# Expert scatter before gather, list products in slot zero, and the order of the last output parts

## The chip, the cores and the metric

The kernel runs on one core of one Trainium2 chip. The metric is the device time of one execution in microseconds (us), smaller being better: 1261.15 us is the median of three executions of the kernel before (1260.3 to 1261.98). The chip's engines are named PE (TensorE, matrix products), DVE (VectorE), ACT (ScalarE), POOL (GpSimd) and SP (SyncE, which here only issues DMAs). Each runs its own instructions strictly in order and waits for others by semaphores.

## The reference, cut to what matters

The input `x` is 4 x 2048 x 256. It is normalised, and two branches read the result; the output is their sum with `x`.

```
xn = layernorm(x)
# attention branch: H = 8 heads, DK = 128, DV = 64, gated linear attention
q, k, v = xn@Wq, xn@Wk / sqrt(DK), xn@Wv ;  alpha = sigmoid((xn@Wg + bg) / 16)
state = alpha*state + k v^T ;  out_t = q . state           # a scan over 2048 tokens
attn  = (out * sigmoid(xn@Wog)) @ Wo
# expert branch: E = 64 experts, 8 chosen per token, at most CAP = 256 tokens per expert
topk  = grouped top-8 of sigmoid(xn @ gate_w.T) + gate_bias
buf[e]= the first 256 tokens that chose e, in token order
y[e]  = (silu(buf[e]@w_gate[e]) * (buf[e]@w_up[e])) @ w_down[e]
ffn[token] += y[e, slot] * weight[token, e]
out   = x + attn + ffn
```

## The kernel before, in words

The 2048 tokens of each batch are cut into C = 16 chunks of 128, and one *step* c = 0..15 handles one chunk of all four batches for the attention. A step has a slot zero (the first projections, and the output projection `out_proj` of the chunk before) and slots s = 1..8, one per head. Other work stands *beside* the attention in fixed places of the slots: every engine has its own function `beside(c, kind, s, place)`, called at numbered places, and this hand-written table alone sets the order.

- Steps 0 to 4, kind "norm": the layer norm and the routing of three chunks each.
- Step 5, "count": counts of the chosen tokens.
- Step 6, "slots": the lists of token numbers, 16 *list products* of four experts each. PE's `slots_of_four` (L777) does the products, DVE's `count_four` (L1479, L1480, L1482, and L1470 for half of the comparisons of a later product) reads them, and POOL's `reach_group` (L659) does the other half of the comparisons. `FOUR_AT` is the table of their (slot, place). They use two banks in turn, and two buffers. At the end of the step `make_lists` (L1492 to L1499) writes the lists, and POOL may gather.
- Steps 7 to 14, "experts": eight experts each, one per slot. For expert e, PE transposes its gathered tokens (`expert_tokens`, L927, at slot e%8 + 1, place 0), makes the hidden layer (L937), and the down product (L948) one slot later. DVE's `expert_out` (L1622) weights the result into the buffer `yb`.
- Step 15, "last": the last chunk. Behind it `out_part` (L914) projects the outputs of chunk 15, in parts by head pairs, batch by batch, and DVE (L1585) adds the rest and SP writes each batch out.

POOL moves the tokens of the experts. `gather(e)` (L627) is two indirect DMAs that read 128 rows of 1280 bytes each from `table`; `scatter(e)` (L635) is two indirect DMAs that add 128 rows of 1024 bytes each to `acc`. PE's `expert_tokens` of e waits for both halves of `gather(e)`. The token buffer `xg` has two halves, so `gather(e + 2)` waits until ACT has read the last of expert e (`share_kept`, L1160). `deliver(e)` waits for DVE's `y_cp`, then until the scatter of the expert before has landed (the rows of two experts may be the same), and then issues `scatter(e)`. For the first expert of a step it first issues `add_attention` (L653), a DMA that adds a chunk's attention output, 512 KB, to `acc`, and waits for its landing (`att_added`). SP loads the experts' weights and the decay tables (`decay`, L405, and `carry`, L411, 512 KB each) on another queue.

Of the kernel before, what the change touches and what calls it, by code (L numbers as in the profile page):

```python
# [23 lines left out]
KO = HV // P  # L24
# [31 lines left out]

COUNT_AT = [(s, 2) for s in range(2, H + 1)] + [(H, 3)]
assert len(COUNT_AT) == E // CB
FOUR_AT = [(s, place) for s in range(1, H) for place in ((0, 4, 2) if s == 4 else (0, 2))] + [(H, 0)]
FOUR_AT.sort(key=lambda at: (at[0], (0, 1, 2, 4, 3).index(at[1])))  # L60
assert len(FOUR_AT) == E // EB
NORM_CHAIN = 3
ROUTE_LINKS = (7, 4, 3, 5)
# [14 lines left out]
def build(nc, x_in, Wq, Wk, Wv, Wo, Wg, bg, Wog, gate_w, gate_bias, w_gate, w_up, w_down, out):  # L78
    with ExitStack() as ctx:
# [281 lines left out]
        def is_last(c):  # L361
            return isinstance(c, int) and c == C - 1
# [191 lines left out]
        def _(pool):  # L554
# [126 lines left out]
                scatter(e)  # L681

            for e in range(E):
                pool.wait_ge(share_kept, e + 1)
                gather(e + 2)
                if e > 0:
                    deliver(e - 1)
            deliver(E - 1)

# [2 lines left out]
        def _(pe):  # L692
# [199 lines left out]
            def out_proj(c, b):  # L892

                to = out_bank(c, b)
                if b == 0:
                    pe.wait_ge(g_low, 4 * c)
                if isinstance(c, int) and c == C - 1:
                    pe.wait_ge((ut_cp, state_up)[b // 2], 4 * (C - 1))
                elif b == 1:
                    pe.wait_ge(state_up, 4 * c)  # L900
                elif b > 1:
                    pe.wait_ge(wo_cp, 4 * (c - 1) + b - 1)
                for j in range(KO):
                    for i, (part, other) in enumerate(PARTS):
                        last = mm(to, gT[:, part, j, b * P:(b + 1) * P], wo[:, other, j, :],  # L905
                                  start=(j + i == 0), stop=(j == KO - 1 and i == 2))
                last.then_inc(wo_ps, 1)
# [70 lines left out]
            def step(c, kind):  # L978
# [13 lines left out]
                proj_qk(c, kind, 0, 1)  # L992
                if not first:
                    out_proj(c, 0)
                proj_v(c, kind, 2)
                if not first:
                    out_proj(c, 1)
                if not is_last(c):
                    keys_back(c, 0)
                scores(c, 0)  # L1000
                if kind in ("experts", "last") and not (isinstance(c, int) and c == E0):
                    expert_down(c - 1, STEP_E - 1)
                proj_v(c, kind, 3)
                if not first:
                    out_proj(c, 2)
                for s in range(1, H + 1):
                    if s > 1 and not is_last(c):
                        keys_back(c, s - 1)
# [41 lines left out]
            step(C - 1, "last")  # L1050
            out_part(2, (0, 1, 2))
            out_part(3, (0, 1, 2))
            out_part(0, (2,))
            out_part(1, (2,))
            for b in range(B):
                out_part(b, (KO - 1,))


        @block.scalar
# [227 lines left out]
        def _(dve):  # L1287
# [338 lines left out]
            def beside(c, kind, s, place):  # L1626
# [29 lines left out]
                if kind == "count" and s > 0:  # L1656
# [2 lines left out]
                            keep_group(COUNT_AT.index((s, pe_place)))  # L1659
                    if place == 3 and s == H:  # L1660
                        keep_totals()
                if kind == "slots" and s == 0 and place == 3:
                    keep_firsts()
                if kind == "slots" and (s, place) in FOUR_AT:
                    count_four(FOUR_AT.index((s, place)))
# [21 lines left out]
            def step(c, kind):  # L1687
                beside(c, kind, 0, 0)
                beside(c, kind, 0, 1)
                if kind != "experts":  # L1690
                    beside(c, kind, 0, 3)
                if kind in ("experts", "last") and not (isinstance(c, int) and c == E0):
                    hidden_low(c - 1, STEP_E - 1)
                    down_low(c - 1, STEP_E - 1)
                if not is_first(c) and not is_last(c):
                    projected(c, 0, kind)
                    projected(c, 1, kind)
                beside(c, kind, 0, 4)
                for s in range(1, H + 1):
                    if kind == "experts":  # L1700
                        keys_weighted(c, s - 1)
# [2 lines left out]
                        expert_out(c - 1, STEP_E - 1)  # L1704
                    if s == 1 and kind == "experts":
                        weights_low_e(c, 0)
                    if s == 1 and not is_first(c) and not is_last(c):
                        projected(c, 2, kind)
                        if kind == "experts":
                            tokens_low_e(c, 0)  # L1710
                        projected(c, 3, kind)
# [76 lines left out]
```

## Time and profile before

| | |
|---|---|
| three executions, median | 1261.15 us |
| the profiled execution's own time | 1266.82 us |
| its span in the trace | 1265.1 us |
| PE busy | 1237.9 us, 98% |
| DVE busy | 976.6 us, 77% |
| ACT busy | 624.3 us, 49% |
| POOL busy | 487.4 us, 39% |
| chain that ended last | PE 76%, DVE 16%, issue 5% |

Times in the rows are microseconds from the span's start. The step "slots" runs from 453.5 to 524.2 us, the first step with experts begins there, and the second runs from 608.2 to 692.1 us. The profiled execution is 5.67 us above the median of the three others. The releaser that a row names behind an idle time is the one that came last by the profile.

### The profile page before, as it was taken

To read this page: it belongs to the slowest core of one execution; us is meant where nothing else is said; L and a number is where in the kernel's file an instruction comes from. 1 tells how busy PE (TensorE), PEld (TensorE's weight loads), DVE (VectorE), ACT (ScalarE), POOL (GpSimd) and SP (SyncE) were. 2 spreads that over 40 slices of the span, in tenths; PEclk is the share of its full clock that TensorE was granted. 3 is DMA by queue.
4 is the path that set the end of the run, shared out by engine and by line. 5 is a ranking of instruction groups with operands and counts; after the bars stand their busy time and mean duration, and the time that the engine had idled before them with its cause. 6 is when DMAs were issued, how large, how long until landed. Compare 5 with 4: busy or idle time off the path is not lost.

```text
span 1265.1 us, 28662 instructions
## 1 busy us (share of the span) xinstructions
PE 1237.9 (98%) x9910; PEld 1092.2 (86%) x9910; DVE 976.6 (77%) x2343; ACT 624.3 (49%) x1319; POOL 487.4 (39%) x377
## 2 busy tenths in 40 slices
PE   7899999999999999999999999999999999999999
PEld 6788888887888888799899998989989999889987
DVE  6997878889797659878688687786885877868844
ACT  6675756666574544344444444444444444434432
POOL 2110111011001027237467385474574754845620
PEclk9999999999999999999999999999999999999999
DMA  6576534354352322357486575674774765748665
GB/s 241 170 250 200 188 110 156 122 190 158 121 171 60 111 75 84 95 145 186 105 198 165 130 178 136 150 181 106 188 171 121 172 155 137 193 104 191 162 194 183
DMA packets 124920, 194.68 MB, mean 154 GB/s; under 512 B 12016, under 2 KB 98608, under 8 KB 124592
## 3 DMA queue, kind: packets, MB, share of 16 engines
q1 hardware_dynamic: 94384, 147.99, 36.1%
q0 software_dynamic: 30464, 45.83, 19.7%
q8 instruction: 34, 0.56, 0.2%
q14 instruction: 38, 0.31, 0.1%
HBM read 148.62 MB, written 57.74 MB: 163 GB/s over the span
## 4 chain that ended last, share of the span: by engine, by line
PE 76%; DVE 16%; issue 5%; ACT 2%; another core or an unknown queue 0%; DVEq 0%; DMA 0%; ACTq 0%
PE bank L793 21%; PE bank L808 7%; PE bank L905 7%; PE bank L937 7%; PE bank L845 6%; PE bank L825 5%; PE bank L877 3%; PE bank L863 3%; PE bank L866 3%; PE bank L948 3%; PE bank L836 3%; DVE Dt L1506 3%; PE bank L889 2%; PE bank L927 2%; DVE At L1527 2%
## 5 line engine op out<-in xcount | busy, mean ns | idle before, releaser
L635 POOL DMA_INDIRECT acc<-arena,idx_all x128 | 224.3, 1752 | 149.4 <-DMA acc<-res 54.1
L627 POOL DMA_INDIRECT arena<-table,idx_all x132 | 163.6, 1240 | 153.8 <-ACT share L1160 96.5
L793 PE MATMUL bank<-xp,wq 128*128 128x512 f32 x768 | 208.4, 406 | 0.0
L793 PE MATMUL bank<-xp,wk 128*128 128x512 f32 x768 | 202.2, 398 | 0.0
L793 PEld LDWEIGHTS bank<-xp,wk 128*128 128x128 f32 x768 | 138.5, 188 | 29.3 <-DVE wk L1416 0.4
L793 PEld LDWEIGHTS bank<-xp,wq 128*128 128x128 f32 x768 | 136.6, 189 | 25.4 <-issue 0.8
L1506 DVE TENSOR_TENSOR_SCAN Dt<-decay,eye_b 128x512 f32<-128x512 f32 x128 | 157.7, 1233 | 0.0
L845 PE MATMUL bank<-qT,kT 128*128 128x128 f32 x1024 | 136.2, 275 | 1.8 <-DVE At L1527 1.4
L1136 ACT ACTIVATE kT<-bank 128x512 f32<-128x512 f32 x128 | 76.7, 599 | 118.0 <-PE bank L793 102.2
L845 PEld LDWEIGHTS bank<-qT,kT 128*128 128x128 f32 x1024 | 125.2, 192 | 3.3 <-DVE At L1527 1.6
L1136 ACT ACTIVATE qT<-bank 128x512 f32<-128x512 f32 x128 | 76.9, 601 | 85.4 <-PE bank L793 64.7
L1527 DVE TENSOR_TENSOR At<-bank,Dt 128x512 f32<-128x512 f32 x128 | 87.7, 685 | 27.9 <-PE bank L845 26.3
L601 POOL DMA_DIRECT2D table<-arena x16 | 12.4, 777 | 248.4 <-DVE arena L1400 232.8
L937 PEld LDWEIGHTS bank<-xgT,wgu_p 128*128 128x128 f32 x768 | 98.6, 188 | 10.4 <-issue 5.7
L863 PE MATMUL bank<-At,V 128*64 128x128 f32 x1024 | 98.7, 273 | 6.4 <-DVE At L1527 6.4
L937 PE MATMUL bank<-xgT,wgu_p 128*128 128x256 f32 x768 | 102.4, 282 | 2.2 <-issue 2.0
L808 PE MATMUL bank<-wv,xp 128*128 128x512 f32 x384 | 103.2, 404 | 0.8 <-DVE xp L1410 0.7
L825 PE MATMUL bank<-xp,wog 128*128 128x512 f32 x384 | 101.8, 400 | 0.0
L905 PEld LDWEIGHTS bank<-wo,gT 128*128 128x128 f32 x720 | 93.3, 188 | 5.5
L905 PE MATMUL bank<-wo,gT 128*128 128x256 f32 x720 | 94.6, 280 | 0.0
L866 PE MATMUL bank<-carry,state 128*64 128x128 f32 x960 | 94.1, 273 | 0.0
L1154 ACT ACTIVATE gT<-gated 128x512 fp32r<-128x512 f32 x64 | 40.4, 630 | 91.5 <-DVE gated L1549 79.1
(174 smaller groups left out, 2317.1 us busy)
## 6 DMA issues: line engine op xcount, KB each, us to landing
decay<-decay_dram SPq DMA_DIRECT2D x64, 512.0 KB
carry<-decay_dram SPq DMA_DIRECT2D x60, 512.0 KB
arena<-in_L_attn_x_dram SPq DMA_DIRECT2D x16, 512.0 KB, 4.5
table<-arena SPq DMA_DIRECT2D x16, 512.0 KB, 3.2
xT_dram<-arena SPq DMA_DIRECT2D x16, 512.0 KB, 3.0
arena<-in_L_ffn_w_gate_dram SPq DMA_DIRECT2D x64, 128.0 KB
arena<-in_L_ffn_w_up_dram SPq DMA_DIRECT2D x64, 128.0 KB
arena<-in_L_ffn_w_down_dram SPq DMA_DIRECT2D x64, 128.0 KB
```

The lines of the kernel that those rows point to most:

```text
L627: pool.indirect_dma_start(out=xg[:, e % 2, j, :], out_offset=None, in_=table[:, :], in_offset=bass.IndirectOffsetOnAxis(ap=idx_all[:, e, j ...
L635: pool.indirect_dma_start(out=acc[:, :], out_offset=bass.IndirectOffsetOnAxis(ap=idx_all[:, e, j:j + 1], axis=0), in_=yb[:, e % 2, j, :], ...
L793: last = mm(to[:, :], w[:, part, k, h * DK:(h + 1) * DK], xp[:, other, k, :], start=(k + i == 0), stop=(k == KD - 1 and i == 2))
L808: last = mm(to[:, :], xp[:, part, k, b * P:(b + 1) * P], wv[:, other, k, :], start=(k + i == 0), stop=(k == KD - 1 and i == 2))
L825: last = mm(to[:, :], wog[:, part, k, j * P:(j + 1) * P], xp[:, other, k, :], start=(k + i == 0), stop=(k == KD - 1 and i == 2))
L845: last = mm(bank[2][:, b * P:(b + 1) * P], kT[:, h % 2, b * P:(b + 1) * P], qT[:, h % 2, b * P:(b + 1) * P], start=True, stop=True)
L863: last = mm(bank[5][u * DV:(u + 1) * DV, b * P:(b + 1) * P], V[:, b, h * DV:(h + 1) * DV], At[:, u, b, :], start=True, stop=is_first(c))
L866: last = mm(bank[5][u * DV:(u + 1) * DV, b * P:(b + 1) * P], state[:, 2 * p + u, b, :], carry[:, p % 2, u, b, :], start=False, stop=True)
L905: last = mm(to, gT[:, part, j, b * P:(b + 1) * P], wo[:, other, j, :], start=(j + i == 0), stop=(j == KO - 1 and i == 2))
L937: last = mm(expert_bank[j % 2][:, m * CAP:(m + 1) * CAP], wgu_p[:, part, m, k * I:(k + 1) * I], xgT[:, other, k * CAP:(k + 1) * CAP], star ...
L1136: f(dst[:, h % 2, :], bank_of(kind, "qk"[which], h)[:, :], ACT.Copy, scale=scale).then_inc(qk_cp, 1)
L1506: dve.tensor_tensor_scan(Dt[:, h, :, :].rearrange("p b t -> p (b t)"), decay[:, (h // 2) % 2, (h % 2) * BP:(h % 2 + 1) * BP], eye_b[:, :, ...
```

## The change

It has three parts, and none changes what is computed.

1. POOL, in the experts' loop: for every expert e except those with e % 8 == 1, `deliver(e - 1)` is called before the wait for `share_kept` and `gather(e + 2)`; before, it was called behind them. With e % 8 == 1 (where `deliver(e - 1)` has the attention's DMA in it) the order stays.
2. The step "slots": four of the 16 list products move into slot zero, at new places 2 to 5 on PE and DVE; the last of them is now at slot 7, place 0. DVE's `keep_firsts` is called at place 1 instead of 3; its place in DVE's order is the same.
3. After the last step PE does parts 2 and 3 of batch 0 together, then of batch 1, then part 3 of batches 2 and 3. Before, part 2 of batches 0 and 1 came first, and then part 3 of all four.

```diff
-FOUR_AT = [(s, place) for s in range(1, H) for place in ((0, 4, 2) if s == 4 else (0, 2))] + [(H, 0)]
+FOUR_AT = [(0, place) for place in range(2, 6)] + [(1, 2)]
+FOUR_AT += [(s, place) for s in range(2, H - 1) for place in (0, 2)] + [(H - 1, 0)]
...
             for e in range(E):
+                slow = e % STEP_E == 1
+                if e > 0 and not slow:
+                    deliver(e - 1)
                 pool.wait_ge(share_kept, e + 1)
                 gather(e + 2)
-                if e > 0:
+                if slow:
                     deliver(e - 1)
...
                 if not first:
                     out_proj(c, 0)
+                beside(c, kind, 0, 2)
                 proj_v(c, kind, 2)
                 if not first:
                     out_proj(c, 1)
+                beside(c, kind, 0, 3)
...
                     projected(c, 0, kind)
+                    beside(c, kind, 0, 2)
                     projected(c, 1, kind)
-                beside(c, kind, 0, 4)
+                beside(c, kind, 0, 3 if kind == "slots" else 4)
...
-            out_part(0, (2,))
-            out_part(1, (2,))
             for b in range(B):
-                out_part(b, (KO - 1,))
+                out_part(b, (2, KO - 1) if b < 2 else (KO - 1,))
```

POOL's order from the first expert on, before. L627 is a gather half, L635 a scatter half, L653 the attention's DMA; in brackets is what the instruction waits for.

```order
L627 DMA arena<-table,idx_all 128x320 [waits share_kept]
L627 DMA arena<-table,idx_all 128x320
L653 DMA acc<-res 128x4x256 [waits init_acc,wo_cp]
L635 DMA acc<-arena,idx_all 8448x256 [waits att_added,y_cp]
L635 DMA acc<-arena,idx_all 8448x256
L627 DMA arena<-table,idx_all 128x320 [waits share_kept]
L627 DMA arena<-table,idx_all 128x320
L635 DMA acc<-arena,idx_all 8448x256 [waits y_cp,scattered]
L635 DMA acc<-arena,idx_all 8448x256
L627 DMA arena<-table,idx_all 128x320 [waits share_kept]
```

These are the gather of expert 3, the attention, the scatter of 0, the gather of 4, the scatter of 1, and the gather of 5 begins. The same place of the kernel after:

```order
L627 DMA arena<-table,idx_all 128x320 [waits share_kept]
L627 DMA arena<-table,idx_all 128x320
L653 DMA acc<-res 128x4x256 [waits init_acc,wo_cp]
L635 DMA acc<-arena,idx_all 8448x256 [waits att_added,y_cp]
L635 DMA acc<-arena,idx_all 8448x256
L635 DMA acc<-arena,idx_all 8448x256 [waits y_cp,scattered]
L635 DMA acc<-arena,idx_all 8448x256
L627 DMA arena<-table,idx_all 128x320 [waits share_kept]
L627 DMA arena<-table,idx_all 128x320
L635 DMA acc<-arena,idx_all 8448x256 [waits y_cp,scattered]
```

The scatter of expert 1 now stands directly behind that of expert 0, and the gather of expert 4 behind both.

PE's order in slot zero of the step "slots" and the slot behind it, before. L905 is `out_proj`, L777 a list product (bank 7 and bank 4 in turn), L808 and L793 projections, L836 and L845 the keys and scores.

```order
L905 MATMUL bank5<-wo,gT 128x256 x12
L808 MATMUL bank0<-wv,xp 128x512 x6
L905 MATMUL bank6<-wo,gT 128x256 x12
L836 MATMUL bank3<-ident,kT 128x128 x4
L845 MATMUL bank2<-qT,kT 128x128 x4
L808 MATMUL bank1<-wv,xp 128x512 x6
L905 MATMUL bank5<-wo,gT 128x256 x12
L777 MATMUL bank7<-arena,sel_all 128x64 x8
L793 MATMUL bank0<-xp,wq 128x512 x6
L905 MATMUL bank6<-wo,gT 128x256 x12
L793 MATMUL bank1<-xp,wk 128x512 x6
L777 MATMUL bank4<-arena,sel_all 128x64 x8
```

And after; each line's number is 3 higher there.

```order
L908 MATMUL bank5<-wo,gT 128x256 x12
L780 MATMUL bank7<-arena,sel_all 128x64 x8
L811 MATMUL bank0<-wv,xp 128x512 x6
L908 MATMUL bank6<-wo,gT 128x256 x12
L780 MATMUL bank4<-arena,sel_all 128x64 x8
L839 MATMUL bank3<-ident,kT 128x128 x4
L848 MATMUL bank2<-qT,kT 128x128 x4
L780 MATMUL bank7<-arena,sel_all 128x64 x8
L811 MATMUL bank1<-wv,xp 128x512 x6
L908 MATMUL bank5<-wo,gT 128x256 x12
L780 MATMUL bank4<-arena,sel_all 128x64 x8
L796 MATMUL bank0<-xp,wq 128x512 x6
```

Four products now stand ahead of the projections of slot 1 (the last row), where before there was one.

## Rows read from the trace of the kernel before

**Rows 1.** The page: busy time of each engine.

```profile
PE 1237.9 (98%) x9910; PEld 1092.2 (86%) x9910; DVE 976.6 (77%) x2343; ACT 624.3 (49%) x1319; POOL 487.4 (39%) x377
```

**Rows 2.** Waits, whole span: waiter, releaser, us in total, times, longest.

```profile
POOL acc L635 <- DMA acc<-res: 54.1, 8, 7.9
```

**Rows 3.** Stretches of two expert steps: PE, PEld, DVE, ACT, POOL busy, clock, DMA.

```profile
608.20:692.10 83.90, 83.90 (x676) 76.06 (x674) 64.73 (x117) 37.81 (x82) 50.23 (x33) 1.00 0.66 157
692.10:777.30 85.20, 84.49 (x674) 75.96 (x672) 64.75 (x117) 37.47 (x82) 51.56 (x34) 1.00 0.65 153
```

**Rows 4.** Timeline of PE, end of step "slots": start, duration, [idle before, releaser].

```profile
521.89 0.44 PE L863 MATMUL bank<-At,V 128*64 128x128 f32 x4 [1.77 <-DVE At L1527]
```

**Rows 5.** Timeline of DVE, same place.

```profile
512.32 0.48 DVE L1470 TENSOR_SCALAR sel_all<-arena 128x256 bf16<-128x256 bf16 x2
...
518.73 0.66 DVE L1479 TENSOR_TENSOR arena<-bank,slot_col 128x504 bf16<-128x504 f32 x1
...
519.42 0.68 DVE L1482 TENSOR_REDUCE arena<-arena 128x8 f32<-128x504 bf16 x1
...
521.15 0.69 DVE L1527 TENSOR_TENSOR At<-bank,Dt 128x512 f32<-128x512 f32 x1
```

**Rows 6.** Timeline, all engines, slot zero of step "slots".

```profile
457.75 3.75 POOL L659 TENSOR_SCALAR sel_all<-arena 128x256 bf16<-128x256 bf16 x4 [46.97 <-DVEq L1463]
...
459.39 1.58 PE L905 MATMUL bank<-wo,gT 128*128 128x256 f32 x12
...
471.08 0.42 DVE L1589 TENSOR_TENSOR res<-bank,addend 128x256 f32<-128x256 f32 x1 [2.71 <-PE bank L905]
```

**Rows 7.** Timeline of POOL, expert step c = 9, experts 0 to 5 of it.

```profile
729.27 2.48 POOL L635 DMA_INDIRECT acc<-arena,idx_all  x1 [6.75 <-DMA acc<-res]
732.06 1.58 POOL L635 DMA_INDIRECT acc<-arena,idx_all  x1 [0.31 <-issue]
...
735.86 1.07 POOL L627 DMA_INDIRECT arena<-table,idx_all  x1 [0.30 <-issue]
737.23 2.37 POOL L635 DMA_INDIRECT acc<-arena,idx_all  x1 [0.30 <-issue]
739.90 1.57 POOL L635 DMA_INDIRECT acc<-arena,idx_all  x1 [0.30 <-issue]
...
743.55 1.54 POOL L627 DMA_INDIRECT arena<-table,idx_all  x1 [0.30 <-issue]
```

**Rows 8.** Timeline, same step: PE's tokens of expert 4, DVE's result of expert 2.

```profile
738.07 0.85 DVE L1622 TENSOR_SCALAR arena<-bank,share 128x256 f32<-128x256 f32 x2
...
743.84 0.60 PE L927 MATMUL bank<-ident,arena 128*128 128x128 f32 x4
```

**Rows 9.** DMA queues, 735.65 to 736.25 (only one has packets): packets, MB, share.

```profile
q1 hardware_dynamic: 198, 0.10, 56.7%
```

**Rows 10.** DMA, 713.2 to 714.0, and POOL's last issue before it.

```profile
DMA packets 0, 0.00 MB, mean 0 GB/s; under 512 B 0, under 2 KB 0, under 8 KB 0
...
710.44 1.07 POOL L627 DMA_INDIRECT arena<-table,idx_all  x1 [0.31 <-issue]
```

**Rows 11.** DMA queues, 743.9 to 748.4, then 748.4 to 750.0.

```profile
q0 software_dynamic: 142, 0.37, 36.4%
...
DMA packets 99, 0.08 MB, mean 53 GB/s; under 512 B 17, under 2 KB 99, under 8 KB 99
```

**Rows 12.** Timeline, step c = 10: POOL's scatter of expert 0, PE's tokens of expert 4.

```profile
816.62 1.55 POOL L635 DMA_INDIRECT acc<-arena,idx_all  x1 [0.31 <-issue]
...
829.14 0.60 PE L927 MATMUL bank<-ident,arena 128*128 128x128 f32 x4
```

**Rows 13.** Timeline, end of the program.

```profile
1257.56 4.49 PE L914 MATMUL bank<-wo,gT 128*128 128x256 f32 x36
...
1259.07 0.69 DVE L1570 TENSOR_TENSOR gT<-gated,gT 128x512 fp32r<-128x512 f32 x1 [0.70 <-ACT gT L1154]
...
1261.49 1.81 SPq L547 DMA_DIRECT2D out_dram<-qT  x4
```

More of the change, by code:

```diff
@@ L58 @@
 assert len(COUNT_AT) == E // CB
-FOUR_AT = [(s, place) for s in range(1, H) for place in ((0, 4, 2) if s == 4 else (0, 2))] + [(H, 0)]
-FOUR_AT.sort(key=lambda at: (at[0], (0, 1, 2, 4, 3).index(at[1])))
+FOUR_AT = [(0, place) for place in range(2, 6)] + [(1, 2)]
+FOUR_AT += [(s, place) for s in range(2, H - 1) for place in (0, 2)] + [(H - 1, 0)]
 assert len(FOUR_AT) == E // EB
@@ L1002, in step @@
                     expert_down(c - 1, STEP_E - 1)
+                beside(c, kind, 0, 4)
                 proj_v(c, kind, 3)
@@ L1005, in step @@
                     out_proj(c, 2)
+                beside(c, kind, 0, 5)
                 for s in range(1, H + 1):
@@ L1661, in beside @@
                         keep_totals()
-                if kind == "slots" and s == 0 and place == 3:
+                if kind == "slots" and s == 0 and place == 1:
                     keep_firsts()
@@ L1689, in step @@
                 beside(c, kind, 0, 1)
-                if kind != "experts":
+                if kind in ("norm", "count"):
                     beside(c, kind, 0, 3)
@@ L1706, in step @@
                         weights_low_e(c, 0)
+                    if s == 1 and kind == "slots":
+                        beside(c, kind, 0, 4)
                     if s == 1 and not is_first(c) and not is_last(c):
                         projected(c, 2, kind)
+                        if kind == "slots":
+                            beside(c, kind, 0, 5)
                         if kind == "experts":
```

## The prediction

> **What bounds the kernel now.** I read the engines' busy times first, then the stretches of single steps, the list of waits, and last the timelines of the three places that the change touches. PE is busy 98% of the span [rows 1]. In an expert step such as c = 8 PE has no idle time at all: 83.90 of 83.90 us [rows 3]. So PE is the bound nearly everywhere. A change pays only where it closes one of the few gaps in PE's order, and whatever makes PE wait in an expert step is added to the end in full. POOL is busy 50 us of such a step [rows 3], and waits some 7 us in each for the attention's DMA (54.1 us in eight) [rows 2]; it has slack on the average, and the question is whether it has it where the gathers are due.
>
> **Part 2, list products in slot zero.** At the end of the step "slots" PE stands 1.77 us until 521.89, waiting for DVE's masked scores At [rows 4]. DVE is why: it comes to At only at 521.15, behind a list product that held it from 518.73 to 519.42 + 0.68 = 520.10 [rows 5]. A list product costs DVE these 1.37 us and 0.48 for two comparisons (L1470) of a later one [rows 5], about 1.9 us in all. Four of them leave slots 1 to 8, so DVE has some 7.6 us less in a stretch at whose end it is about 2 us late. The stall goes; next in line is then PE's own order. What takes the four in? In slot zero DVE waits for each of the four `out_proj`, 2.71 us for the last of them [rows 6]; if the others are like it, 7.6 us fit into these 10. PE comes to the first product after the `out_proj` of 459.39, that is at 460.8. It needs POOL's comparisons, four instructions from 457.75 in 3.75 us, of which two are done by 459.6 and four by 461.5 [rows 6]; PE's second product is due past 463.5. No wait. The third needs POOL again after the first product, two instructions or 1.9 us, from 461.3 to 463.3, due at about 465.4. I take -2.2 us: the 1.77 and 0.2 to 0.6 of smaller gaps that the late DVE causes. Bounds: -3.0 if DVE's lateness costs PE more than the rows show, and +0.5 if the products wait in slot zero.
>
> **Part 3, the last parts.** 36 products take 4.49 us from 1257.56 [rows 13], so the first 18 end near 1259.8. DVE's last low half is ready at 1259.07 + 0.69 = 1259.76. Before, six more products (0.7 us) stood between the two; now PE meets that wait just as it ends, and may lose 0.1 us. In return batch 0 is complete three products earlier, 0.36 us minus the wait; SP issues the four outputs in 1.81 us, one after another [rows 13], and could start up to 0.3 us sooner, but batch 3 still comes last of all 36. I take 0; bounds -0.3 and +0.2.
>
> **Part 1, POOL.** The order was: scatter 0, gather 4, scatter 1, gather 5 (numbers of the experts within a step). It becomes scatter 0, scatter 1, gather 4. Nothing is added, but a gather now stands behind a scatter that waits for two things: the result of the expert before, and the landing of the scatter before. I follow it through step c = 9.
>
> - The scatter of 0 is late in every step, since POOL waits for the attention's DMA (6.75 us), and it starts at 729.27; its second half is issued at 732.06 [rows 7]. By 735.65 it has landed: from there to 736.25 the DMA engines carry only the other queue's packets [rows 9].
> - Before, the gather of 4 used this time: its second half was issued at 735.86 [rows 7]. Now POOL stands still until the landing, about 735.6, and starts the scatter of 1 some 1.2 us after it, my estimate of how fast POOL answers a landing; a direct bound is the row itself, in which it started at 737.23 without waiting. So at 736.9.
> - That scatter took 737.23 to 741.47, 4.2 us, because its first half lasted 2.37 instead of about 1.6 [rows 7]; DVE's `expert_out` at 738.07 lies inside it [rows 8], and will again. So it ends at 741.1.
> - The gather of 4 is then issued from 741.4, its second half 1.4 to 1.8 us later, at 743.0. That is nearly where the gather of 5 stands today (second half at 743.55 [rows 7]).
> - It lands at best 2.7 us later: a gather half issued at 710.44 had landed by 713.2, from when there are no packets at all [rows 10]. At worst as the gather of 5 does today: issued at 743.55, its bytes (0.33 of the 0.37 MB) pass until 748.4, and behind that only packets of 0.8 KB, a scatter's [rows 11], which makes 4.8 us. So it lands between 745.7 and 747.8.
> - PE wants it at 743.84 less the weight load, 743.7 [rows 8]. Today it is there in time. Then PE stands 2.0 to 4.1 us.
>
> I take a lag of 3.4 us, nearer to the free case than to the loaded one, because the loaded case has a 512 KB load of SP beside it whose hour may shift: a stall of 2.6 us. How many of the eight steps are like c = 9? POOL's wait for the attention is 54.1 / 8 = 6.76 us in the mean [rows 2] against 6.75 here, so c = 9 is the middle and I count five like it. The other three I take to be like c = 10: the second half at 816.62, the tokens at 829.14, so 12.5 us between them against 11.8 in c = 9 [rows 7, 8, 12], and the scatter of 1 took only 3.5 us there; I give these 0.5 us each (0 to 2). Sum: 5 x 2.6 + 3 x 0.5 = 14.5 us. For the later gathers of a step (5, 6, 7) POOL is no longer behind the attention, and PE's stall at 4 has moved their due time too; I add nothing, with 0.5 us per step as the upper bound. What queues behind PE's wait is everything of PE; DVE and ACT get the time to catch up. In the traced run some expert steps have more gaps than others, as the 1.3 us by which c = 9 is longer than c = 8 [rows 3]. If a stall ahead of such gaps swallows 1.1 us in two of the eight steps, that is -2.2 us; the bounds are 0 and -5.
>
> The Trainium skill ("DMA: Bandwidth & Descriptors", section "Anatomy of one DMA — SWDGE (gpsimd) path") puts a POOL-issued DMA at about 2.0 us plus its bytes at 436 GB/s. For a gather half of 164 KB that is an estimate of 2.4 us; rows 10 agree (2.7), rows 11 (4.8, beside SP's load) do not. By the page the stall would be 1.7 us and five of them 8.5 instead of 13.
>
> **The sum.** In the profiled execution: -2.2 + 0 + 14.5 - 2.2 = +10.1 us, from 1266.82 to about 1276.9. That execution is 5.67 us above the median of the three others; the same +10.1 on 1261.15 gives 1271.
>
> **The rivals.**
>
> - *The gathers still come in time.* If the gather of 4 reaches PE before it asks, parts 2 and 3 alone are left. For it speaks that DVE's `expert_out` may hit POOL's instructions less when a scatter starts right behind it, and that without a profiler the transfers may be quicker. It decides at one place: if scatter 1 and gather 4 together come 2 us (c = 9, free case) sooner than I reckon. Against it: even with 1.6 us per scatter half, 1.1 per gather half and a lag of 2.7 the chain from the landing at 735.6 is 1.2 + 3.5 + 0.3 + 1.4 + 2.7 = 9.1 us, and PE asks after 8.1. Time: 1261.15 - 2.2 to -4.4, about 1258.5. The page "SBUF — State Buffer" of the Trainium skill (section "Who interferes with whom") says that some DVE operations lock POOL out of a shared port; rows 7 and 8 look like it, but the scatter of 1 meets `expert_out` in both orders.
> - *A small stall.* All at the lower ends: five stalls of 0.5 to 1.0 us cancel part 2. Time 1260 to 1264.
> - *The whole loop is late.* If every lag is the loaded one (4.1 us in five steps, 1.5 in three) and gathers 5 to 7 come late as well, 20.5 + 4.5 + 4 - 2.2 = +27: 1288.
> - *Slot zero only moves the stall.* The list products wait there for POOL or DVE, so part 2 brings nothing: +12 instead of +10, 1273. Rows 6 leave 1 us of slack at each place against it.
>
> **How the numbers follow.** Forecast (a stall at the tokens of 4, with or without the gain of slot zero): 0.64. The whole loop late: 0.10. Small stall: 0.11. In time: 0.15. Predicted 1271. The range leaves out the upper half of the late loop and the lower part of the in-time case: 1259 to 1284; the forecast's own range is 1264 to 1281. A change of 0.2%, 2.5 us, is about what can be told from none. Slower by more than that: 0.64 + 0.10 + 0.04 of the small stall, 0.78. Within it: 0.07 of the small stall and 0.02 of the in-time case, 0.09. Faster: 0.13.
>
> **What would show it.** At PE's tokens of each step's fifth expert (L927, now L930) a wait for a DMA of 1.5 to 4 us, eight times or at least five, and POOL idle ahead of each step's second scatter with "DMA acc" as the releaser. The expert steps then grow from 84 to about 86 us. The wait of 1.77 us for At at the end of the step "slots" is gone, and the next step starts some 2 us sooner. The prediction is wrong if PE does not wait for a gather at all, if that wait stands at another expert, or if PE stands in slot zero of the step "slots".

## The result and the profile after

The changed kernel takes 1274.65 us (median of 6 runs, 1271.71 to 1278.64), the kernel before 1261.02 (6 runs, 1260.28 to 1261.98). The ratio is 1.0112, interval 1.0103 to 1.0122: 1.1% slower. Forecast was 1271. The traced execution is the longest of the six: 1278.64 us, span 1277.0, against 1266.82 and 1265.1 before. So +13.6 us by the medians and +11.8 from profile to profile; the section on the prediction shows why the two differ.

The page after, the row of busy times, to set beside [rows 1]:

```profile
PE 1240.1 (97%) x9910; PEld 1094.9 (86%) x9910; DVE 979.0 (77%) x2343; ACT 624.3 (49%) x1319; POOL 477.4 (37%) x377
```

The engines do the same work. PE's idle time is 1277.0 - 1240.1 = 36.9 us against 27.2 before. The list of waits (waiter, releaser, us in total, times, longest) says for what PE waits:

```profile
POOL acc L635 <- DMA acc<-res: 55.6, 8, 7.5
...
PEld bank L930 <- DMA arena<-table,idx_all: 17.2, 11, 5.6
PE bank L930 <- DMA arena<-table,idx_all: 15.1, 11, 5.4
```

The first row is that of [rows 2], nearly unchanged (55.6 against 54.1 us): POOL is as late from the attention's DMA as before. The other two are new. L930 is PE's tokens, `arena<-table` a gather: weight load and matmul of the same tokens wait eleven times, up to 5.6 us. (The two rows are one wait seen on PE's two queues and are not added.)

The windows from one step's first tokens to the next's, for c = 8, 9 and 10 (columns as in [rows 3]):

```profile
621.80:706.84 85.04, 84.32 (x675) 76.07 (x674) 64.87 (x117) 37.62 (x81) 47.97 (x34) 1.00 0.66 155
706.84:792.48 85.64, 84.07 (x675) 76.04 (x674) 65.09 (x117) 37.63 (x81) 49.12 (x34) 1.00 0.65 153
792.48:884.47 91.99, 86.60 (x675) 78.00 (x674) 64.95 (x117) 37.64 (x81) 48.66 (x34) 0.96 0.61 143
```

A step without a gap takes 83.85 us (shown below). c = 8 has 1.2 us more, c = 9 has 1.8, and c = 10 has 8.1 with a granted clock of 0.96.

Now the place followed in the prediction. Timeline of POOL in c = 9, then PE's row at its end, to be read against [rows 7, 8]:

```profile
729.20 2.60 POOL L635 DMA_INDIRECT acc<-arena,idx_all  x1 [6.81 <-DMA acc<-res]
732.11 1.58 POOL L635 DMA_INDIRECT acc<-arena,idx_all  x1 [0.31 <-issue]
736.80 1.56 POOL L635 DMA_INDIRECT acc<-arena,idx_all  x1 [3.12 <-issue]
738.67 1.55 POOL L635 DMA_INDIRECT acc<-arena,idx_all  x1 [0.30 <-issue]
740.53 1.12 POOL L627 DMA_INDIRECT arena<-table,idx_all  x1 [0.30 <-issue]
741.95 1.27 POOL L627 DMA_INDIRECT arena<-table,idx_all  x1 [0.30 <-issue]
```

```profile
743.00 1.06 PE L848 MATMUL bank<-qT,kT 128*128 128x128 f32 x8
745.63 0.66 PE L930 MATMUL bank<-ident,arena 128*128 128x128 f32 x4 [1.57 <-DMA arena<-table,idx_all]
```

Both halves of the scatter of expert 0 start when they did before (729.27 and 732.06), then POOL stands 3.12 us. The profile writes "issue" there, but what POOL waits for is `scattered`, the landing of the scatter before. At the same place of c = 8, 12 and 14 the profile names it:

```profile
650.16 1.56 POOL L635 DMA_INDIRECT acc<-arena,idx_all  x1 [3.06 <-DMA acc<-arena,idx_all]
```

In the trace's semaphore counts the last count of `scattered` comes 0.84 to 0.85 us before POOL starts again, at this place of all eight steps. Before, the gather of 4 stood in this hole (second half 735.86). Now it goes out at 741.95 and is in PE's hands at 745.63, 3.7 us later; PE stands 1.57 us. DVE's `expert_out` is at 738.13.

The same in c = 10, where the wait is longest. POOL, then PE, then the windows ahead of the wait, inside it and behind it:

```profile
816.76 2.65 POOL L635 DMA_INDIRECT acc<-arena,idx_all  x1 [7.41 <-DMA acc<-res]
819.72 1.96 POOL L635 DMA_INDIRECT acc<-arena,idx_all  x1 [0.31 <-issue]
825.57 1.56 POOL L635 DMA_INDIRECT acc<-arena,idx_all  x1 [3.89 <-issue]
827.44 1.90 POOL L635 DMA_INDIRECT acc<-arena,idx_all  x1 [0.30 <-issue]
829.65 1.13 POOL L627 DMA_INDIRECT arena<-table,idx_all  x1 [0.30 <-DMA acc<-arena,idx_all]
831.09 1.07 POOL L627 DMA_INDIRECT arena<-table,idx_all  x1 [0.30 <-issue]
```

```profile
828.64 1.06 PE L848 MATMUL bank<-qT,kT 128*128 128x128 f32 x8
835.09 1.12 PE L930 MATMUL bank<-ident,arena 128*128 128x128 f32 x4 [5.39 <-DMA arena<-table,idx_all]
```

```profile
816.00:829.00 13.00, 13.00 (x122) 11.97 (x122) 10.34 (x20) 6.11 (x14) 7.74 (x4) 1.00 0.51 114
829.50:833.80 4.30, 0.20 (x2) 0.01 (x1) 2.86 (x6) 0.36 (x1) 2.32 (x3) 1.00 1.03 274
833.80:840.70 6.90, 5.61 (x16) 4.57 (x17) 1.88 (x2) 1.29 (x3) 5.24 (x4) 0.51 0.53 87
840.70:850.00 9.30, 9.30 (x63) 8.43 (x62) 6.94 (x12) 4.10 (x10) 5.42 (x4) 1.00 0.40 80
```

It is the same chain with nearly every link longer. Against the time at which PE asks (the end of the row ahead of the tokens, 744.06 and 829.70), scatter 0 starts 14.9 us ahead in c = 9 and 12.9 in c = 10 (1.9 lost up to there, 0.6 of it in the longer wait for the attention's DMA); from its second half to scatter 1 it is 4.69 us and 5.85 (1.2 more); that pair takes 3.73 and 4.08, gather and landing 5.10 and 5.44 (0.7 more). Together 3.8 us, the difference of the waits (5.39 - 1.57). And PE's granted clock, 1.00 until 833.8, is 0.51 for 6.9 us, the 1.2 GHz level, after PE had done nothing since 829.7; c = 10 is 91.99 us long, 8.1 over 83.85: 5.6 of wait (by the weight loads) and 2.5 more.

Part 2: the end of the step "slots", DVE and then PE (beside [rows 4, 5]):

```profile
518.64 0.69 DVE L1532 TENSOR_TENSOR At<-bank,Dt 128x512 f32<-128x512 f32 x1 [0.98 <-PE bank L848]
```

```profile
517.47 1.06 PE L848 MATMUL bank<-qT,kT 128*128 128x128 f32 x8
518.93 1.09 PE L880 MATMUL bank<-kw,V 128*64 128x128 f32 x16 [0.40 <-ACT kw L1084]
519.85 0.39 PE L866 MATMUL bank<-At,V 128*64 128x128 f32 x4
```

DVE now waits for PE's scores and not the other way round, and the first gap left on PE is 0.40 us for ACT's `kw`. By the weight loads the step of the first expert begins at 536.0 instead of 538.4, 2.4 us sooner.

### The profile page after: what moved, and what is told of

It reads as the page before. It is cut to its first block and busy times, and to the rows that moved or that the text cites. A ratio compares the mean times of both kernels' runs of the same rounds, so it can differ in the third digit from the quotient of the medians.

```text
span 1277.0 us, 28660 instructions
## 1 busy us (share of the span) xinstructions
PE 1240.1 (97%) x9910; PEld 1094.9 (86%) x9910; DVE 979.0 (77%) x2343; ACT 624.3 (49%) x1319; POOL 477.4 (37%) x377
## 5 line engine op out<-in xcount | busy, mean ns | idle before, releaser
L635 POOL DMA_INDIRECT acc<-arena,idx_all x128 | 215.7, 1685 | 222.7 <-DVE arena L1627 98.2
L627 POOL DMA_INDIRECT arena<-table,idx_all x132 | 164.7, 1248 | 107.2 <-issue 47.4
L869 PE MATMUL bank<-carry,state 128*64 128x128 f32 x960 | 94.2, 273 | 0.0
L1145 ACT ACTIVATE V<-bank 128x512 f32<-128x512 f32 x64 | 38.2, 597 | 95.2 <-PE bank L811 95.2
```

The costliest lines, as they stand in the source:

```text
L627: pool.indirect_dma_start(out=xg[:, e % 2, j, :], out_offset=None, in_=table[:, :], in_offset=bass.IndirectOffsetOnAxis(ap=idx_all[:, e, j ...
L635: pool.indirect_dma_start(out=acc[:, :], out_offset=bass.IndirectOffsetOnAxis(ap=idx_all[:, e, j:j + 1], axis=0), in_=yb[:, e % 2, j, :], ...
L869: last = mm(bank[5][u * DV:(u + 1) * DV, b * P:(b + 1) * P], state[:, 2 * p + u, b, :], carry[:, p % 2, u, b, :], start=False, stop=True)
```

## The experiments

The theory that I went in with is called A in the expectations: behind the attention's DMA POOL is late, two scatters now stand next to each other, the second waits for the landing of the first with nothing to fill the wait, and the gather behind them reaches PE late. The other letters are its rivals, named where they stand. Each run has the kernel before beside it on its chip; "the fifth expert" is the one whose gather stood between the scatters of 0 and 1. Waits of single experts are gaps between PE's weight loads ahead of the tokens, good to about 0.1 us.

**The three parts apart.** Part 1 alone, on the kernel before:

```diff
+                slow = e % STEP_E == 1
+                if e > 0 and not slow:
+                    deliver(e - 1)
                 pool.wait_ge(share_kept, e + 1)
                 gather(e + 2)
-                if e > 0:
+                if slow:
                     deliver(e - 1)
```

> Part 1 alone on the kernel before. If the loss is PE's wait for the fifth expert's gather of each step (theory A), this is the changed kernel less the gain of the lists: PE waits for a gather at L927 by 15 to 18 us in all, at the fifth expert of all eight steps, and the time is 1275 to 1279. Rival B, the slot-zero products or their knock-on in the expert steps carry a part of the loss: then it is clearly under the 1274.65 of the changed kernel.

1279.63 us (4 runs, 1275.96 to 1281.63) against 1260.84: 1.0140, interval 1.0124 to 1.0155. The cost is all of part 1: 18.8 us against 13.6 of the whole change. Part 2's missing gain makes 2.5 of the difference; the other 2.7 aren't explained. The expectation had the waits at the fifth expert alone. In the trace that expert waits in all eight steps, 12 us in all, and the sixth and the eighth wait too, in three and six steps, another 7 us. The wait for At stands again (PE, end of "slots"), and the list names the gathers:

```profile
521.53 0.44 PE L866 MATMUL bank<-At,V 128*64 128x128 f32 x4 [1.78 <-DVE At L1530]
```

```profile
PE bank L930 <- DMA arena<-table,idx_all: 15.6, 16, 5.0
```

Part 2 alone:

```diff
-FOUR_AT = [(s, place) for s in range(1, H) for place in ((0, 4, 2) if s == 4 else (0, 2))] + [(H, 0)]
+FOUR_AT = [(0, place) for place in range(2, 6)] + [(1, 2)]
+FOUR_AT += [(s, place) for s in range(2, H - 1) for place in (0, 2)] + [(H - 1, 0)]
...
```

> Part 2 alone. Theory A: 2.0 to 2.6 us faster than the kernel before, 1258.5 to 1259.0; PE's wait of 1.77 us for At at the end of the step of the lists is gone, no wait for a gather anywhere. Rival B: the same time as before or slower, since slot zero or the first expert step take the 2.4 us back.

1258.31 us (11 runs, 1257.99 to 1258.87) against 1260.84: 0.9981, interval 0.9972 to 0.9990. It gains 2.5 us, and beats both kernels. The window of an expert step (token to token) shows a step with no gap at all, the 83.85 us used above; all seven steps that have another behind them are like that, and the eighth has no wait.

```profile
619.65:703.50 83.85, 83.85 (x675) 76.06 (x674) 64.67 (x117) 37.63 (x81) 48.21 (x33) 1.00 0.65 158
```

Part 3 alone:

```diff
-            out_part(0, (2,))
-            out_part(1, (2,))
             for b in range(B):
-                out_part(b, (KO - 1,))
+                out_part(b, (2, KO - 1) if b < 2 else (KO - 1,))
```

> Part 3 alone. Forecast 0 (-0.3 to +0.2): 1260.8 to 1261.2. A rival in which batch 0 leaving earlier lets SP's four outputs start sooner gives -0.3, one in which PE meets DVE's last low half gives +0.2; PE's last 36 products then take 4.49 us with a gap inside.

1260.9 us (11 runs) against 1260.84: 1.0001, interval 0.9992 to 1.0010. Nothing.

**Moving the place at which the order changes.** From here on the diffs are against the changed kernel. Gather first for the experts 1 and 2 of a step:

```diff
-                slow = e % STEP_E == 1
+                slow = e % STEP_E in (1, 2)
```

> The changed kernel with the gather first for the third expert too (e % 8 == 2, the iteration that issues the gather of the step's fifth expert). Theory A: the scatter of expert 1 starts at the same time, but the fifth expert's gather uses the wait for the landing: the waits at the fifth expert go (15 us), the sixth expert gets at most 0.5 us in some steps, and the time is 1258.5 to 1262. Rival C, POOL or the DMA engines are late over the whole step whatever the order: the wait moves to the sixth or seventh expert and the time stays over 1268.

1277.06 us (4 runs, 1275.22 to 1278.32) against 1260.84: 1.0126, interval 1.0110 to 1.0141. The expectation failed: what came is what it gives for rival C. The fifth expert has no wait any more, but the sixth has one in seven of eight steps (2.9, 1.6, 1.5, 1.6, 1.5, 1.8, 1.4, 0), and so has the eighth, 0.3 to 1.3. POOL in c = 9 of it, and PE at the sixth expert:

```profile
739.78 1.63 POOL L635 DMA_INDIRECT acc<-arena,idx_all  x1 [0.30 <-issue]
741.72 1.79 POOL L635 DMA_INDIRECT acc<-arena,idx_all  x1 [0.30 <-issue]
747.94 1.56 POOL L635 DMA_INDIRECT acc<-arena,idx_all  x1 [4.43 <-DMA acc<-arena,idx_all]
749.80 1.56 POOL L635 DMA_INDIRECT acc<-arena,idx_all  x1 [0.30 <-issue]
751.66 1.64 POOL L627 DMA_INDIRECT arena<-table,idx_all  x1 [0.30 <-issue]
753.61 1.63 POOL L627 DMA_INDIRECT arena<-table,idx_all  x1 [0.30 <-DMA acc<-arena,idx_all]
```

```profile
757.24 0.66 PE L930 MATMUL bank<-ident,arena 128*128 128x128 f32 x4 [1.17 <-DMA arena<-table,idx_all]
```

This is the hole of c = 9 after, moved one expert on, and here the profile names the releaser. So the harm is not tied to the attention's expert as such. At both places tried it stands where the order turns from gather-first to scatter-first while POOL is still behind. The theory in that form is A2, which says in addition that the turn is harmless where POOL idles.

> The changed kernel with the gather first for e % 8 in 1 to 5. The run before it only moved the wait from the fifth to the sixth expert, so the theory now reads (A2): where the order switches from gather-first to scatter-first two scatters stand next to each other, and the landing of the first is a wait of POOL that no gather fills; while POOL is behind from the attention's DMA this makes the next gather late, and later in the step, when POOL idles anyway, it costs nothing. A2: no wait of PE for a gather over 0.5 us, 1258.0 to 1260.0. Rival C (scatter-first is too slow for any expert, since the gather then starts 4 us after the result): waits of PE at experts 7 and 8 of each step, 0.5 to 1 us each, 1263 to 1270.

```diff
-                slow = e % STEP_E == 1
+                slow = 1 <= e % STEP_E <= 5
```

1258.37 us (11 runs, 1257.96 to 1259.0) against 1260.38: 0.9984, interval 0.9976 to 0.9993. No PE row for a gather is left in its list of waits. POOL's wait for the landing is still there, and at the turn (the scatter of 5 behind that of 4) it is 3.3 to 6.5 us, against 3.0 to 3.9 in the changed kernel. It costs nothing there:

```profile
POOL acc L635 <- DMA acc<-arena,idx_all: 40.2, 11, 6.5
```

A2 held, and rival C fell: the gathers behind the turn are in time. Since part 2 alone is as fast (on another chip, each against the kernel before beside it), scatter-first brings nothing where it does no harm.

**Taking links out of the chain.** The attention's DMA out (its addition is left undone, the order stays):

```diff
-                pool.dma_start(acc_tiles[c - 1], res[:, :, :], accum_op=ALU.add).then_inc(att_added, 16)
+                pool.nop().then_inc(att_added, 16)
```

> The changed kernel without the attention's DMA into acc (eight DMAs of 512 KB are left out, POOL's wait for their landing with them); everything else and the order stay. A2: POOL issues the scatter of a step's first expert some 7 us earlier, is never behind, and PE never waits for a gather: 1257.5 to 1259.5. Rival C: the waits at the later experts stay, 0.5 to 1 us at two or three of a step: 1263 to 1275. Rival D, the DMA engines' load is the cause: the fifth expert still waits by the lag of its gather, only less.

1260.15 us (11 runs, 1258.14 to 1261.33) against 1260.38: 0.9997. The waits at the fifth expert are gone, in all eight steps, and the trace has none of those that rivals C and D gave. The median is 0.7 us above what I had written, and the traced run, the fastest, shows no gap over 0.1 us; where the others lose 2 us isn't known.

The wait for the landing out (odd experts are added to a second table, so that a scatter waits only for the one before the last; that table is not joined to the result):

```diff
-                        out=acc[:, :], out_offset=...
+                        out=(acc, acc_b)[e % 2][:, :], out_offset=...
...
-                        compute_op=ALU.add).then_inc(scattered, 16)
+                        compute_op=ALU.add).then_inc(scattered[e % 2], 16)
...
-                if e > 0:
-                    pool.wait_ge(scattered, 16 * NHALF * e)
-                    pool.nop().then_inc(yb_free, 1)
+                if e > 1:
+                    pool.wait_ge(scattered[e % 2], 16 * NHALF * (e // 2))
...
-                dve.wait_ge(yb_free, e + 1)
+                wait_past(dve, scattered[j % 2], 16 * NHALF * ((c - E0) * (STEP_E // 2) + j // 2))
```

> The changed kernel, in which the results of odd experts are added to a second table that is read by nobody (the output lacks them), so that a scatter waits for the landing of the scatter two before instead of the last. The attention's DMA stays, and waits for both. A2: the second scatter of a step starts 3 us earlier, directly behind the first, so its fifth expert's gather is 3 us earlier: the eight waits there shrink from 1.9 (0.7 in some) to under 0.5, 1258.5 to 1262. Rival C, POOL's own time for scatter and gather is what is missing: the waits stay over 1 us, over 1266.

1259.2 us (11 runs, 1258.46 to 1260.61) against 1260.38: 0.9992, interval 0.9983 to 1.0001. POOL in c = 9, from the scatter of 0 to the gather of 4:

```profile
725.96 1.64 POOL L637 DMA_INDIRECT acc<-arena,idx_all  x1 [6.72 <-DMA acc<-res]
727.90 1.56 POOL L637 DMA_INDIRECT acc<-arena,idx_all  x1 [0.31 <-issue]
729.76 1.56 POOL L637 DMA_INDIRECT acc_b<-arena,idx_all  x1 [0.30 <-issue]
731.63 1.59 POOL L637 DMA_INDIRECT acc_b<-arena,idx_all  x1 [0.30 <-issue]
733.53 1.12 POOL L629 DMA_INDIRECT arena<-table,idx_all  x1 [0.30 <-issue]
```

The order and the lateness (6.72 us) are those of the changed kernel; what is missing is the hole. (DVE's wait for the buffer `yb` changes with it, last lines of the diff.) The gather starts 7.6 us after the scatter of 0, against 11.3 (729.20 to 740.53) with it: 2.8 us are the hole (3.12 less the usual 0.30) and 1.0 the shorter first half. PE doesn't wait at that place any more (0.1 us at most in any step); the eighth expert still waits in three steps, 0.3, 0.3 and 0.8 us. This run shows the landing wait to be a link without which there is no stall: scatter-first without it is within 0.1% of part 2 alone (0.9992 and 0.9981, each against the kernel before on its chip).

The attention's DMA issued earlier, behind the gather of a step's first expert, so that POOL goes on while it lands:

```diff
             def deliver(e):
-                if e % STEP_E == 0:
-                    add_attention(E0 + e // STEP_E, e)
...
                 gather(e + 2)
+                if e % STEP_E == 0:
+                    add_attention(E0 + e // STEP_E, e)
```

> The changed kernel, with the attention's DMA issued one iteration earlier (behind the gather of the step's third expert instead of behind that of the fourth), so that it lands about when the first expert's result is there. A2: POOL's wait for it falls from 6.8 us to 0 to 2 in each step, and PE's waits for gathers are gone: 1258 to 1260. Rival: the earlier DMA, 512 KB read and added, waits on POOL for the output projection's last part and holds the gather of the fourth expert; then PE waits there instead and the time is over 1264.

1261.15 us (12 runs, 1260.2 to 1266.19) against 1260.38: 1.0011, interval 1.0003 to 1.0020. One microsecond over the expectation. The traced execution took 1265.6 us, 4.4 over the median, so it shows more than most of them have. In it the fifth expert's waits are gone but for one of 0.3 us, and so is POOL's row for `acc<-res`; but in four steps the eighth expert waits, once 2.61 us:

```profile
937.23 1.04 PE L930 MATMUL bank<-ident,arena 128*128 128x128 f32 x4 [2.61 <-DMA arena<-table,idx_all]
```

In this execution the lateness has a second place, at the end of a step. It isn't taken further here.

**Scatter first for one expert of eight only, and the changed kernel again.** If the turn is all, one turn is enough to cause the waits:

```diff
-                slow = e % STEP_E == 1
+                slow = e % STEP_E != 2
...
-                if slow:
+                if slow and e > 0:
```

> The changed kernel with the scatter first for e % 8 == 2 alone, so that the scatters of a step's experts 1 and 2 are adjacent and everything else is as before. A2 (adjacency while POOL is late is the whole loss): the fifth expert waits 0.7 to 2 us in each step as in the changed kernel, no other expert waits, and the time is 1267 to 1273, most of the loss of 1274.65. Rival C (the later experts' thin margin carries it): 1258.5 to 1262.

1282.36 us (5 runs, 1281.23 to 1286.12) against 1263.57 on this chip: 1.0150, interval 1.0132 to 1.0169. That is 9 us over the upper end of the expectation and slower than the change itself. The waits for gathers are as A2 has them: at the fifth expert in every step, four of about 1.9 us and four of about 0.4. But they make only 9 of the 24 us by which its span is over that of part 2 alone (1280.7 against 1256.3). The expectation also said that everything else is as before, and that isn't so: behind the turn the order turns back, and the gathers of 4 and 5 stand next to each other, four halves in a row and the scatter of 2 behind them, which no other kernel has at this place. And the list of waits has a long row that most of the other kernels lack:

```profile
DVE gated L1554 <- remote: 26.1, 9, 4.3
```

One such place, c = 8: POOL, then DVE.

```profile
660.77 1.02 POOL L627 DMA_INDIRECT arena<-table,idx_all  x1 [0.30 <-issue]
662.10 1.62 POOL L635 DMA_INDIRECT acc<-arena,idx_all  x1 [0.30 <-issue]
```

```profile
659.15 0.42 DVE L1614 TENSOR_TENSOR wde_p<-arena,wde_p 128x256 fp32r<-128x256 f32 x1
663.79 0.69 DVE L1554 TENSOR_TENSOR gated<-bank,og 128x512 f32<-128x512 f32 x1 [4.22 <-remote]
```

DVE stands 4.22 us with no releaser that the profile names; ACT and PE then run late behind it. It starts just behind POOL's scatter half (662.10 + 1.62 = 663.72), but that is so at only three of the nine places. What DVE waits for here is `oi_ps`, which PE counts up with its product L869. The trace's semaphore counts have this count at 663.76, where the profile ends the product at 658.76 (PE's ends are modelled). At the nine places the count is 1.9 to 5.0 us behind that end, against 0.02 in the median. So DVE waits for PE's count. Whether the products themselves ended so late, or their counts alone were held up, and by what, isn't shown, and most of this run's time stays open.

Three of the twelve traces have such late counts: this one, the one of the run below (the row says 8.0 us, 5 times), and the traced execution of the kernel before. In the other nine none is over 0.3 us late. For the kernel before the row is

```profile
DVE gated L1549 <- remote: 6.4, 4, 2.1
```

and its four places lie in c = 9, 10, 11 and 13, the steps of that trace that are 1.1 to 1.45 us over 83.85. The late counts are thus not a matter of one order of POOL alone.

> The changed kernel once more, beside the one above and on the same chip. 1272 to 1278; in its profile the fifth expert's waits come in all eight steps. If one of them exceeds 5 us as in c = 10 of the first profile, the granted clock is low in the stretch behind it; without so long a wait it stays at 1.00 throughout the expert steps.

The changed kernel, unchanged, on the same chip: 1272.58 us (8 runs, 1267.51 to 1284.11) against 1263.57 (13 runs, 1261.63 to 1266.2): 1.0078, interval 1.0050 to 1.0106. The kernel before is itself 2.7 us slower here than in the first runs on this chip (1260.84), which isn't explained. In its traced execution, the longest, the fifth expert's waits are 5.3, 2.0, 0, 4.7, 2.0, 0.7, 1.9, 0.1, so they come in six steps and not, as expected, in all eight. Behind the one of 5.3 the clock is low again. Windows over that wait and behind it, then behind the wait of 4.7 in c = 10:

```profile
571.00:577.00 6.00, 2.34 (x24) 1.98 (x20) 5.00 (x10) 1.08 (x3) 5.07 (x4) 1.00 0.85 194
577.30:584.10 6.80, 5.75 (x16) 4.70 (x17) 1.82 (x2) 1.29 (x3) 3.04 (x3) 0.50 0.52 109
840.10:843.50 3.40, 2.78 (x9) 2.40 (x10) 1.00 (x2) 0.69 (x2) 2.79 (x3) 0.50 0.84 137
```

The last row is behind a wait under 5 us, where the expectation had 1.00. The kind of wait belongs to the kernel. The long one stands in c = 10 in all three traces of this order of POOL (5.6 here first, 5.2 with part 1 alone, 4.7 now), and in c = 7 too in this one, so its place is partly the kernel's and partly the execution's. It isn't made by the hole: here and with part 1 alone the second scatter starts the usual 4.6 to 4.7 us behind the first one's second half, but the gather takes 4.9 to 5.5 us from its second half to PE.

One thing sets the four long waits apart from the other 20 steps of the three traces: SP's next loads (three blocks of weights and `decay`, 0.9 MB together) come first. The first of them is issued 1.1 to 3.0 us ahead of the gather's second half, and in the other steps 0.5 to 1.2 us behind it. In the 4 us from that second half on SP's queue then moves 0.7 to 0.8 MB, and 0.3 to 0.45 in the other steps. This is the loaded case of the prediction, which had 4.8 us for it. It is a coincidence in four of four cases and no experiment; what puts the loads ahead isn't shown. The spread of the times is 17 us here, 5 for the kernel before.

## Why the prediction was right, and where its sizes were off

The prediction was right in sign, in place and in mechanism: POOL stands still until the landing of the scatter of 0, the gather of 4 goes out where that of 5 did, and PE waits at each step's fifth expert. It could be checked against what it named, point by point.

- *The wait.* Forecast 1.5 to 4 us at the fifth expert in at least five of eight steps. Measured 1.9, 0.6, 1.8, 5.6, 2.1, 0.7, 1.9, 0.7 in c = 7 to 14: there in all eight, in five of them over 1.5. Sum 15.3 us against 14.5. But the makeup differs: the middle kind is 1.9, not 2.6, the loose kind 0.7, not 0.5, and one wait of 5.6 makes up for it. c = 10, which I had taken for a model of the loose kind from [rows 12], is the long one.
- *The chain in c = 9.* Start of scatter 1: forecast 736.9, measured 736.80. The answer of POOL to a landing, my estimate of 1.2 us, was right: from the last packet of the scatter of 0 (735.61) to 736.80 it is 1.19. The releaser "DMA acc" is named in three of the eight steps, "issue" in five. The pair: forecast 4.2 us, measured 3.4 (736.80 to 740.22). That was the failing step of this chain: I wrote that `expert_out` lies inside the first half and will again lengthen it to 2.37; it ran at 738.13, when 1.33 us of that half were over, and the halves took 1.56 and 1.55. Gather of 4, second half: forecast 743.0, measured 741.95. Lag: taken 3.4, measured 3.7.
- *The rule on POOL's DMAs.* The 2.4 us which the prediction worked out from the Trainium skill ("DMA: Bandwidth & Descriptors", section "Anatomy of one DMA — SWDGE (gpsimd) path") are not borne out here: where PE waited for the fifth expert, it took 3.2 to 4.1 us from the second half's start to PE's matmul in the eight steps (3.7 in c = 9). The rows decide.
- *Waits at other experts.* Taken at nothing, with 0.5 us per step as the bound: 2.5 us in all (c = 8 seventh, c = 12 sixth and eighth).
- *The clock.* Not in the sum: 2.5 us behind the long wait.
- *Part 2.* Forecast -2.2; measured -2.4 in the profile (536.0 against 538.4) and -2.5 alone. It didn't only move the stall. *Part 3.* Forecast 0; measured 0.0.
- *The absorbed gaps.* Forecast -2.2. The seven whole steps of the profile before add up to 593.2 us, 6.2 more than seven of 83.85. I read these as gaps of the kernel. They were gaps of that one execution, most of them (5.4 us) in the four steps in which PE's count reaches DVE late (above): the runs of part 2 alone, of part 3 alone and with the turn behind expert 5 have steps of 83.85 us only, and part 3 alone has the time of the median before. So in the profile 6.2 us went away, and in the medians nothing was there to go.

The sum, profile to profile: -2.4 + 15.3 + 2.5 + 2.5 - 6.2 = +11.7, and +11.8 were measured. The forecast was +10.1. In the medians it is another sum: the last term falls away, since the median before has no such gaps (it is 5.8 us under its traced execution), and the median after is 4.0 us under its own, so in most executions the waits and the clock should come to about 4 us less than in the trace (worked out from the times, not seen in a trace). That leaves 11.8 + 5.8 - 4.0 = +13.6. The term of the sum that was mis-sized is thus the last, applied to a median that never held it; without it the forecast for the median would have been 1273.5. That the first sum, of 14.5 for the fifth expert, came so near is in part luck: four waits of about 1.9 us stand where the forecast had five of 2.6, and the one long wait, in a step counted as loose, made up for the rest.

Of the rivals, "in time" and "a small stall" fell with the first wait. "The whole loop is late" was partly right (some waits at later experts), far from its size. "Slot zero only moves the stall" fell with part 2 alone.

What stays open: why single steps have waits of 5 us (the links of c = 10 add up to it, and in all four SP's loads are ahead of the gather, but no run moved these loads); what makes PE's counts late in three of the traces, and so most of the time of the one-turn kernel; and where the kernel without the attention's DMA loses 2 us in most runs.

## What to carry to other kernels

Between two transfers of which the second waits for the landing of the first, an independent one is worth its place: here the gather cost nothing there, and taken out it left a hole that ends with the landing. When the order of a queue is turned somewhere in a loop, look at what becomes adjacent at the turn, and turn it where the queue idles. And before a term is taken from the extra length of one traced execution, set that execution against the median; what the median doesn't hold can't be gained or absorbed there. When a row says "remote" or "issue", look up in the kernel what the instruction waits for before the nearest neighbour in time is blamed.

## What the runs showed of the hardware

- A scatter of two halves of 128 rows holds the next one up for 4.6 to 5.9 us from the start of its second half in the eight steps of the changed kernel (4.7 from 732.11 to 736.80, 5.9 from 819.72 to 825.57), and for 4.9 to 8.3 us at the turn of the kernel with gather first for five experts. POOL starts again 0.84 us after the last count, 1.2 us after the last packet. The fifth expert's gather is in PE's hands 3.2 to 4.1 us after the issue of its second half starts, and 4.9 to 5.5 us in the three steps of the two other traces in which SP's loads were ahead of it.
- The wait of PE costs more than its length where it is long. Behind the one of 5.4 us the granted clock was 0.51 for 6.9 us (1.2 GHz), which cost 2.5 us more. With gather first for two experts it was 0.50 for 3.4 us behind the wait of 2.9 (the row below), and that step took 88.27 us: 83.85 + 2.9 of wait + 1.5. With the attention's DMA issued earlier it was 0.51 for 3.4 us behind the wait of 2.61. Behind the waits of about 2 us it stayed at 1.00.

```profile
584.40:587.80 3.40, 3.40 (x12) 2.82 (x11) 1.82 (x2) 0.82 (x3) 2.79 (x3) 0.50 1.03 244
```

- A half of the same scatter takes 1.56 us or up to 2.65 on POOL. In the trace of the kernel before, the 22 halves with DVE's `expert_out` wholly inside them take 2.34 us in the mean, the 98 with none of it 1.63. The long first half at 729.20 has it inside (730.27 to 731.12), as the one of [rows 7, 8] does; in c = 9 after it ran only 0.2 us into the second scatter's half, and this was short. The 2.65 us at 816.76 have no `expert_out` inside, and their cause stays open.
- In three of the twelve traces PE's count of `oi_ps` reaches DVE up to 5.0 us behind the end that the profile gives the product, with 0.02 to 0.03 in the median. The cause is not shown.
